# Block-window attention with FFN on one core: values ahead of scores, output projections one slot sooner, and the softmax maximum as a ScalarE bias in the last four slots

## What is computed

```python
xw   = blocks of 16 queries; keys/values: the first token plus 3 blocks (own and two before), masked
sim  = (x Wq * 64**-0.5) (x Wk)^T                    # 16 x 49 useful columns, masked above the diagonal
attn = softmax(sim)                                  # maximum subtracted
attn = einsum('gh,bhnij->bgnij', w_th, attn)         # heads mixed after the softmax
o    = (attn (x Wv)) Wo + b_out
x1   = layernorm(x + o)
h    = gelu(rms_norm(x1) ternary(w_up)^T)            # 128 -> 512
y    = layernorm(x1 + rms_norm(h) ternary(w_down)^T)
```

## Time and profile before

| | us |
|---|---|
| median of 3 runs (241.25 to 242.36) | 241.5 |
| the profiled execution, its own time | 243.09 |
| its span in the profile | 241.3 |
| busy in it: TensorE matmul / DVE / ScalarE / GpSimd | 226.1 / 176.6 / 164.1 / 92.6 |
| scores of slots 12, 16, 20, 24, 28 begin at | 82.06, 106.91, 132.92, 158.88, 185.08 |

### The profile page before, as it was taken

How to read it: one execution, slowest core, us unless ns; L and a number is a source line. 1 busy time by engine, 2 the same in 40 slices (tenths; PEclk the granted TensorE clock), 3 DMA queues, 4 the chain that set the end, 5 groups by cost and what they waited for, 6 DMA issues and landing times.

```text
span 241.3 us, 10011 instructions
## 1 busy us (share of the span) xinstructions
PE 226.1 (94%) x4343; PEld 203.1 (84%) x4343; DVE 176.6 (73%) x461; ACT 164.1 (68%) x311; POOL 92.6 (38%) x111
## 2 busy tenths in 40 slices
PE   7999899999999999999999999999999989989970
PEld 7899789888999999888988998888988977889750
DVE  0674699987777882688766885688468999785864
ACT  2686466776666648985599559964898334988652
POOL 7035204531343342444515454536254353120542
PEclk9999999999999999999999999999999999999975
DMA  6937560020020001100200111010201001000002
GB/s 217 293 101 209 165 139 7 7 61 3 3 58 13 24 3 39 35 21 8 65 3 4 48 34 36 3 46 4 68 3 29 20 3 46 1 4 22 3 3 87
DMA packets 19107, 11.69 MB, mean 48 GB/s; under 512 B 2232, under 2 KB 18168, under 8 KB 18936
## 3 DMA queue, kind: packets, MB, share of 16 engines
q1 hardware_dynamic: 18324, 10.47, 15.3%
q10 hardware_dynamic: 740, 0.59, 0.8%
HBM read 8.91 MB, written 2.10 MB: 46 GB/s over the span
## 4 chain that ended last, share of the span: by engine, by line
PE 57%; DVE 15%; ACT 8%; issue 7%; POOL 6%; SPq 2%; DMA 2%; POOLq 0%; DVEq 0%; ACTq 0%
PE bank L1108 9%; PE bank L1110 8%; PE bank L1109 8%; PE bank L1257 7%; PE bank L1231 6%; PE bank L1215 4%; DVE CTl L876 4%; POOL gTl L533 2%; DVE AT L881 2%; POOL xw L506 2%; DMA raw<-in_L_attn_x 2%; SPq L395 2%; DVE sm L896 2%; PE bank L1327 2%; PE bank L1189 2%
## 5 line engine op out<-in xcount | busy, mean ns | idle before, releaser
L577 ACT ACTIVATE Yb<-bank 128x512 f32<-128x512 f32 x64 | 38.4, 601 | 28.4 <-PE bank L1110 27.9
L519 POOL TENSOR_TENSOR E<-E,rc 128x400 f32<-128x400 f32 x32 | 27.9, 871 | 77.3 <-DVE rc L898 77.3
L876 DVE TENSOR_TENSOR CTl<-bank,CTh 128x512 fp32r<-128x512 f32 x64 | 41.1, 683 | 22.3 <-ACT CTh L577 22.1
L1108 PE MATMUL bank<-xTh,Gh 128*128 128x256 f32 x128 | 39.4, 308 | 1.7 <-ACT Yb L577 1.5
L1108 PE MATMUL bank<-CTh,Mh 128*128 128x256 f32 x128 | 37.0, 289 | 0.6 <-DVE CTl L876 0.6
L577 ACT ACTIVATE CTh<-bank 128x512 fp32r<-128x512 f32 x64 | 34.8, 600 | 2.5 <-PE bank L1257 2.4
L1110 PE MATMUL bank<-CTh,Ml 128*128 128x256 f32 x128 | 36.1, 282 | 0.0
L724 ACT ACTIVATE E<-E 128x400 f32<-128x400 f32 x32 | 17.3, 541 | 27.5 <-DVE E L890 27.4
L1109 PE MATMUL bank<-CTl,Mh 128*128 128x256 f32 x128 | 36.0, 281 | 0.0
L1109 PE MATMUL bank<-xTl,Gh 128*128 128x256 f32 x128 | 35.8, 280 | 0.0
L1110 PE MATMUL bank<-xTh,Gl 128*128 128x256 f32 x128 | 35.7, 279 | 0.0
(11 more groups left out here) (142 smaller groups left out, 469.3 us busy)
## 6 DMA issues: line engine op xcount, KB each, us to landing
raw<-in_L_attn_x SPq DMA_DIRECT2D x37, 64.0 KB
pt_rows<-PT SPq DMA_DIRECT2D x2, 512.0 KB, 4.7
R<-pt_rows SPq DMA_DIRECT2D x1, 1024.0 KB, 5.6
xr<-in_L_attn_x SPq DMA_DIRECT2D x6, 128.0 KB
out<-y SPq DMA_DIRECT2D x6, 128.0 KB, 1.9
raw<-in_L_attn_x SPq DMA_DIRECT2D x13, 56.0 KB
w_sb<-in_L_attn_w_qkv SPq DMA_DIRECT2D x2, 256.0 KB, 4.7
w_sb<-in_L_attn_w_qkv ACTq DMA_DIRECT2D x2, 256.0 KB, 4.5
```

Source lines behind the costliest of these rows:

```text
L519: tt(e, e, rc[s % 2][:, :].unsqueeze(2).broadcast_to([P, TILES, WIN]), ALU.mult).then_inc(s_norm, 1)
L577: copy = lambda o, i, **k: nc.scalar.activation(o, i, ACT.Copy, **k)
L876: v.tensor_tensor(ct_view(CTl[s // 4 % 2], s % 4, q), c_view(s, q), ct_view(f32(CTh[s // 4 % 2][:, :, :]), s % 4, q), ALU.subtract).then_i ...
L1108: mm(o, wh, rh, start=start, stop=False, **k)
```

## The change

Constants: `O_LAG` is 6, `TURN` 7, `BIASED` 28. From slot 8 on TensorE does `c_part(s-2)`, `scores(s)`, `transposes(s-1)`, the FFN's pieces, `queries(s, 0)`, `o_part` number `s-6`, `down`, `queries(s, 1)`. Slot 7 turns from the old order to the new one and does two projection parts; slot 31 also does two. `FIRST` is 10, 14, 18, 22, 26, 30, so each FFN step comes a slot sooner, chunk 4 stays in the loop until its square sum, and the special placements of chunks 3 and 4 are gone. `square_sum` stands inside `scores`, ahead of the mask matmul. GELU follows the exp directly. From slot 28 on DVE only changes the maximum's sign, and ScalarE computes exp straight from bank 0 in eight instructions, one per tile, with that as the bias; scores then wait for the exp of the slot before. The tail is rewritten, with 30 filler matmuls (`keep_busy`) where there were 5.

The tables:

```diff
-O_LAG = 7
+O_LAG = 6
+TURN = 7
+BIASED = 28
...
-            if s < 28:
-                return [divmod(s - O_LAG, 4)] if s >= O_LAG else []
-            return {28: [(5, 1), (5, 2)], 29: [(5, 3)], 30: [(6, 0)], 31: []}[s]
-        FIRST = [11 + 4 * n for n in range(5)] + [30]
+            if s < TURN:
+                return []
+            early = {7: [(0, 0), (0, 1)], 31: [(6, 1), (6, 2)]}
+            return early.get(s, [divmod(s - O_LAG, 4)])
+        FIRST = [10 + 4 * n for n in range(6)]
```

ScalarE's loop, slot s:

```diff
-                if s > LAG:
+                if LAG < s <= TURN:
                     ct_hi(s - LAG - 1)
...
+                if s >= TURN:
+                    ct_hi(s - 2)
+                    at_hi(s - 1)
...
                 act.wait_ge(s_sub, s + 1)
-                nc.scalar.activation(e, e, ACT.Exp).then_inc(s_exp, 1)
-                if s >= O_LAG:
+                if s < BIASED:
+                    nc.scalar.activation(e, e, ACT.Exp).then_inc(s_exp, 1)
+                else:
+                    for tile in range(TILES):
+                        ins = nc.scalar.activation(E[s % 2][:, tile, 0:WIN], bank[S_BANK][:, WIN * tile:WIN * tile + WIN],
+                                                   ACT.Exp, bias=mx[s % 2][:, tile:tile + 1])
+                    ins.then_inc(s_exp, 1)
+                for n, k in ffn(s):
+                    if k == 2:
+                        gelu(n, 0)
+                        gelu(n, 1)
+                if s >= TURN:
                     y_out(s, 1)
```

DVE, in `shift(s)` and then in its loop:

```diff
-                v.tensor_tensor(E[k][:, :, 0:WIN], scores, mx[k][:, :].unsqueeze(2).broadcast_to([P, TILES, WIN]),
-                                ALU.subtract).then_inc(s_sub, 1)
+                if s < BIASED:
+                    v.tensor_tensor(E[k][:, :, 0:WIN], scores, mx[k][:, :].unsqueeze(2).broadcast_to([P, TILES, WIN]),
+                                    ALU.subtract).then_inc(s_sub, 1)
+                else:
+                    v.tensor_scalar(mx[k][:, :], mx[k][:, :], -1.0, None, ALU.mult).then_inc(s_sub, 1)
...
+                if s > TURN:
+                    ct_lo(s - 2)
+                shift(s)
                 for n, k in ffn(s):
-                    if k == 5 and n == 3:
+                    if k == 5:
+                        dve.wait_ge(f_back, n + 1)
                         hidden_sum(n)
+                if s >= TURN:
+                    at_lo(s - 1)
```

TensorE, `scores` and its loop:

```diff
-            def scores(s):
+            def scores(s, sums=()):
                 need(pe, s_sub, s)
+                if s > BIASED:
+                    pe.wait_ge(s_exp, s)
...
+                for n in sums:
+                    pe.wait_ge(f_dS, n + 1)
+                    square_sum(n)
...
-                if s >= LAG:
+                if LAG <= s <= TURN:
                     transposes(s - LAG)
-                scores(s)
+                if s > TURN:
+                    c_part(s - 2)
+                scores(s, [n for n, k in ffn(s) if k == 5])
+                if s > TURN:
+                    transposes(s - 1)
...
-                if s >= LAG:
+                if LAG <= s < TURN:
                     c_part(s - LAG)
```

TensorE's tail behind `up` of chunk 6, old and new order:

```diff
-            attn_back(7)
-            down(4)
-            down(5)
-            down_back(4)
-            square_sum(4)
-            down(6)
-            down_back(5)
-            x1_T(7)
-            square_sum(5)
-            down_back(6)
-            up(7, 0)
-            up(7, 1)
-            square_sum(6)
-            keep_busy(2, 5)
+            down(5)
+            attn_back(7)
+            down_back(5)
+            square_sum(5)
+            keep_busy(1, 4)
+            down(6)
+            square_sum(6)
+            keep_busy(1, 4)
+            x1_T(7)
+            down_back(6)
+            keep_busy(1, 6)
+            up(7, 0)
+            up(7, 1)
+            keep_busy(1, 16)
             down(7)
             square_sum(7)
             down_back(7)
```

More of the change, by code:

```diff
@@ L310, in ss_bank @@
             return bank[O_BANK] if n >= 5 else dn_bank(n)
-        def c_bank(s, q):
-            return bank[(0, 2)[q] if s == 30 else C_BANK[q]]
         def y_bank(s, b):
@@ L318, in squared @@
         def squared(n):
-            return gT[0] if n < 4 else gT[2] if n % 2 else gsq
+            return gT[0] if n < 5 else gT[2] if n % 2 else gsq
         def gset(n):
@@ L345, in c_view @@
         def c_view(s, q):
-            return c_bank(s, q)[:, :].rearrange("p (r h s) -> p r h s", r=2, s=BLK)
+            return bank[C_BANK[q]][:, :].rearrange("p (r h s) -> p r h s", r=2, s=BLK)
         def f32(ap):
@@ L547, in _ @@
                 for n, k in ffn(s):
-                    if k == 4 and n < 4:
+                    if k == 4:
                         hidden_low(n, 0)
@@ L736, in _ @@
                         x1_hi(n)
-                    if k == 3 and n < 4:
+                    if k == 3:
                         hidden_high(n, 0)
                         hidden_high(n, 1)
-                    if k == 2 and n < 4:
-                        gelu(n, 0)
-                        gelu(n, 1)
-                    if k == 8 and n < 3:
+                    if k == 8:
                         result(n)
-            at_hi(30)
-            ct_hi(29)
-            gelu(4, 0)
+            x1_hi(5)
+            ct_hi(30)
             at_hi(31)
-            ct_hi(30)
-            gelu(4, 1)
+            stage(6)
             ct_hi(31)
-            x1_hi(5)
-            stage(6)
-            hidden_high(4, 0)
-            hidden_high(4, 1)
-            squares(4, 0)
-            squares(4, 1)
             gelu(5, 0)
@@ L762, in _ @@
             hidden_high(5, 1)
-            result(3)
             x1_hi(6)
+            result(4)
             squares(5, 0)
             stage(7)
+            squares(5, 1)
             gelu(6, 0)
@@ L770, in _ @@
             hidden_high(6, 1)
-            down_out(4)
-            squares(5, 1)
             down_out(5)
@@ L1018, in _ @@
                         up_input(n)
-                shift(s)
-                for n, k in ffn(s):
-                    if k == 5 and n < 3:
-                        hidden_sum(n)
-                    if k == 5 and n == 3:
-                        second_sum(n)
-                    if k == 6 and n == 3:
-                        second_norm(n)
-                    if k == 0 and n == 5:
-                        residual(n)
                 if s == STEPS - 1:
@@ L1256, in c_part @@
                             row = slice(64 * q, 64 * q + WIN)
-                            ins.append(mm(c_bank(s, q)[:, col], xw[s // 4 % 2][row, m, c, :], AT[row, a, col],
+                            ins.append(mm(bank[C_BANK[q]][:, col], xw[s // 4 % 2][row, m, c, :], AT[row, a, col],
                                           start=(n == 0), stop=(n == 2)))
@@ L1344, in _ @@
             for s in range(STEPS):
-                if 0 < s < O_LAG:
+                if 0 < s < TURN:
                     queries(s, 0)
@@ L1360, in _ @@
                         attn_back(n)
[L1361 removed]
+                    if k == 2:
                         up(n, 0)
                         up(n, 1)
[L1364 removed]
+                if s == 0 or s >= TURN:
                     queries(s, 0)
[L1366 to L1369 removed]
+                if s == TURN:
                     pe.wait_ge(s_eva, read_no("A", "m", 3))
@@ L1373, in _ @@
                     o_part(*part)
+                    if part == (0, 0):
+                        c_part(s - 2)
+                        transposes(s - 1)
                 for n, k in ffn(s):
-                    if k == 4 and n < 4:
+                    if k == 4:
                         down(n)
```

94 lines of the change are left out of this document (37 added, 57 removed).

## The result

The changed kernel takes **262.0 us** (median of 4 runs, 259.9 to 263.9), the kernel before beside it 241.9 (4 runs, 241.3 to 242.9): ratio 1.080, 95% interval 1.069 to 1.090. The forecast had the sign and the mechanism right and the size wrong: 254.4 was forecast, 12.9 over the median of 241.5 that it went by; 262.0 came, 20.0 over the 241.9 beside it and beyond the range's upper end of 259.5. Ratios are of fast runs alone, which leaves out one slow run of the changed kernel (without it the median is 260.6), three of e6 (241.0) and one of e9 (257.3).

What follows compares the result with a forecast made beforehand. TensorE, busy 94% of the span, was taken as the bound. Middle 5.9, slots 28 to 31 3.05 and 1.9, tail 0.1 and clock 2.0 sum to +12.9 over 241.5: 254.4 us, range 246.5 to 259.5.

Steps and rivals of the forecast that it cites:

- +2.66: At any slot's scores, values 0.91, a projection part 1.44 and FFN 0.31 more are done: work moved, no loss.
- +5.9: Middle slots: 9.3 us of added waits at `down` less 3.4 us of removed gaps.
- GpSimd's queue is where this collides: `hidden_low` stands directly behind the high half that awaits raw rows; `down` waits 4.1, 1.1, 1.1 and 3.0 us.
- Rivals 3 and 4: 3: GpSimd's collision hidden, only the end pays, 243, chance 0.08. 4: faster, TensorE alone bounds, 237.3, chance 0.07.
- rival 1: The stalls come but the clock stays at 2.4 GHz: 252.4 us, chance 0.28.
- rival 2: Clock falls in three places and loads cost more, or DVE and GpSimd slow each other: about 258 us, chance 0.12.
- one fall, a bit shorter: TensorE's clock is taken to fall once because of the stalls, costing +2.0 us; bounds 0 and 7.8.
- A fall costs at most 2.6 us: Upper cost of one clock fall, from 5.2 us of slower transposes at the kernel's start.
- at least as empty: Stalls of 4.1 and 3.0 us, and slots 29 and 30, compared with the tail microsecond where the clock falls.
- `down` at 16.65: Windows 5 and 6: TensorE reaches `down` 16.65 us into slot 16's or 20's count, so waits 1.1 each.
- 3.05 and 1.9: Slots 28 to 31: +3.05 us from added waits, +1.9 from chunk 4's FFN work ahead of the last projection.
- it starts 9.3 after the projection's end, not 7.0 (+2.3): Tail: last `up` starts 2.3 us later relative to the projection, the rest is 2.15 shorter; net +0.1.

Runs made afterwards that it cites:

- e6: e4 with chunk 4's GELU made a plain copy, so without its table loads: 241.5 us, ratio 0.9953.
- e9: The changed kernel with only the tail edits of e5: 258.6 us, ratio 1.0639.
- e3: The changed kernel with 26 filler matmuls ahead of `down` in slots 14 and 26: 256.6 us, ratio 1.0602.
- e1: The changed kernel with GpSimd's high half of windows 3 to 7 one slot later, behind `hidden_low`: 245.5 us, ratio 1.0145.
- e4: The changed kernel with the edits of e1 and e2 together (late high half, no bias part): 244.6 us, ratio 1.011.
- e5: e4 with the tail reordered on TensorE and ScalarE and ten fillers fewer: 239.4 us, ratio 0.9875.
- e2: The changed kernel with only the bias part undone (VectorE subtracts the maximum, one exp per slot): 259.3 us, ratio 1.0692.

## Why the prediction was right in kind and wrong in size

The profiled execution's 17.5 us, cut at three points that both traces have (scores of slots 12 and 28, end of the last chunk's projection, which is where the prediction cut as well):

| stretch | before | after | change | forecast |
|---|---|---|---|---|
| to scores of slot 12 | 82.06 | 84.02 | +2.0 | +2.66 |
| to scores of slot 28 | 103.0 | 115.25 | **+12.2** | +5.9 |
| to the projection's end | 35.1 | 36.5 | +1.4 | +2.3 |
| to the end of the span | 21.1 | 23.0 | **+1.9** | +0.1 |
| clock, wherever it falls | | (in the rows above) | | +2.0 |

**The collision was read rightly.** Waits of 4.1, 1.1, 1.1 and 3.0 were forecast, from start to start. Measured in the same way, e3 less e1, they are 4.0, 2.2, 1.4 and 3.1: 10.8 against 9.3 in all. The step "GpSimd's queue is where this collides" stands, by the trace and by e1: it needed only the order of one queue and the fact that the fetch waits for the low half. Rivals 3 and 4, in which that wait is hidden or never comes, fall, and so does rival 1, with a clock that stays up. The second half of rival 2, that VectorE and GpSimd slow each other, has no support: GpSimd's pieces take 2.39 to 2.41 and 2.49 to 2.51 us, before 2.40 and 2.55. Window 4 came 1 us sooner than I had it (high half at 100.44, not 101.4), since slot 12 itself stood 0.7 earlier.

**The failed step is the clock's +2.0: "one fall, a bit shorter".** It fell in slot 14 *and* in slot 26, in slot 30, and in the tail. By e3 the first two cost 2.1 and 2.5, the one in the tail 1.1 and the one in slot 30 nothing here: 5.7 in all, where 2.0 stood. "A fall costs at most 2.6 us" held, with some luck; the count did not. The 2.6 is half of some 5 us of slower transposes at the kernel's start, whose granted-clock rows read 1.00, and the two falls of the middle lasted 6.8 us each, so that they could have cost more. I had written that the two long stalls, and slots 29 and 30, were "at least as empty" as the place in which the clock falls in the kernel before, and then charged for one. By the rows there was no reason to count the second at nothing, as both were of one size in the end (2.90 and 2.57 in one piece). Rival 2 had the three places and a chance of 0.12; even its 258 was too low, because what the waits and the tail cost beyond the forecast was missing as well. The Trainium skill's rule ("TensorE: Matmul & The Clock Gate", Part 1), that idleness takes the clock away and sustained work gives it back, agrees with the trace here: the long waits did cost, each time.

**The middle without the clock was 7.2, not 5.9.** In e3, in which the clock is full, it takes 110.3. The waits are the whole of the 1.3: 10.8 less the 3.5 of gaps that e1 shows won is 7.3. Nearly all of the miss is in slots 18 and 22. The low halves came when forecast (16.9 and 18.2 us into slot 16 were forecast, TensorE's two steps start at 17.0 and 18.2), but "`down` at 16.65" is wrong: TensorE was there at 15.8 in slot 16's count and 15.7 in slot 20's, about 0.9 sooner, and waited so much longer. That the return transposes ahead of the hidden sum cost nothing is nearly borne out: e1 has the same order, and its middle is shorter than before by all of the gaps, with four small waits of 0.21 to 0.24 for the low weights in it.

**Slots 28 to 31: forecast +2.3 (3.05 and 1.9, less the 2.66 done sooner), measured +1.4; the pieces roughly right.** Values of slot 28 waited 1.68 (forecast 1.6), scores 0.41 (0.6), the projection 0.65 (0.55), and the transposes 0.42 to 0.50 (0.75 and 0.7); the wait of 0.75 for scores 31 did not come, but stands in e3 with 0.71. Eight exps took 1.65 (forecast 1.8). That GELU 4 between two exps is worse than the bias is not shown: the medians say so (3.1 in e6 against 0.9 in e4 beside e1), but the traces, up to the projection's end and with no fall in e4 and e6, have 1.2 for the GELU's tables and 2.5 for the bias. The page of the Trainium skill that spoke against this part harder, "ScalarE: Activation LUTs", What ACT_TABLE_LOAD costs, with a drain of 1.38 us behind each load, is again not borne out: the load at 203.68 ends at 204.96, and GELU starts at 204.97.

**The tail was costed at +0.1 and lost 1.9, and a better order recovers 3.8 of it.** The step that failed is "it starts 9.3 after the projection's end, not 7.0 (+2.3). From there on [...] 12.05 to the end, not 14.2 (-2.15)". It started 10.5 after it, and 12.5 were left. In e3, where the clock does not fall in the tail, the two are 9.8 and 12.1: the fall is 1.1 of the miss, and the work and waits ahead of the last `up` 0.5. I summed work there and did not look at ScalarE's queue, where `down_out(5)` stands behind chunk 6's halves and makes TensorE wait 1.59 (239.61). In the order of e5 and e9 the last `up` starts 7.0 after the projection's end.

**Between the profiled execution and the medians** lie 2.5 us more (20.0 against 17.5). The profiled execution of before lies 1.2 above the median beside the change (1.6 above the one that the forecast used); that of after lies 1.3 below its own. The changed kernel's runs spread over 4.0 us, those of before beside them over 1.7. Falls that come and go are the likely cause: the windows of e9 and the change at 160 show one that comes in one execution and not in another, and the time goes with each run's mean clock. The change's two slowest runs (263.3 and 263.9) have 0.943 and 0.950, its two fastest 0.954 and 0.978, and e4's ten part into two groups in the same way. Which falls the other executions had is not shown, as they have no trace. Waits at `down` are not needed for it: e1 and e4 have none and spread by 3.2 and 3.4 us; e5, whose tail has lost the wait of 1.59, spreads by 0.55.

Shares of the change by medians, each from its own experiment, so that they overlap and do not add up, with what the traces have in brackets: the order on GpSimd's queue with what it does to the clock 16.5 (15.8 in the middle), of the clock alone 5.4 (5.7); the tail 3.4 to 5.2 (3.8 to 4.1); GELU 4 between exps 3.1 (1.2); the bias 0.9 to 2.7 (1.5 to 2.5). They come to more than 20 because the order is sound once they are mended: e5 is 2.8 us faster than the kernel before.

## What to carry to other kernels

Moving a step one slot sooner moves it past everything on each queue that it uses: look for the instruction on that queue that waits for a transfer, and put nothing behind it that TensorE needs soon. Cost each idle stretch of TensorE of some 3 us twice, once as the wait and once as the clock behind it (2.1 and 2.5 us here), and count every such stretch. When two medians differ by less than their runs spread, compare the traces stretch by stretch, and look where the clock fell in each. When the middle has changed, read the tail's order again: what its last chain hangs on should be next in the queue when it is ready.

## What the runs showed of the chip that I had not expected

- A wait of 2.6 to 2.9 us in one piece, in the middle of dense work, brought the 1.2 GHz level for 6.8 us each, 2.1 and 2.5 us of time. In e2 waits of 2.9 and 3.1 brought it for 3.4 us each (from 104.2 and from 189.5). 26 matmuls of fillers (3.27 us) in the wait's place kept the clock at 1.00 and took nothing from the kernel.
- In e4 a wait of 1.99 in slot 30 left the clock alone, in e5 the same wait of 1.99 brought it down from about 193.8 to 197.2; in e1 and the change 1.67 and 1.68 brought it down, in e3 1.67 did not. So a wait of this size can go either way; no run here settles on what that hangs.
- What a fall costs depends on what else sets the pace. With the bias, a fall in slot 30 cost nothing (36.6 us up to the projection's end in e1 with it and in e3 without). Without the bias it cost 0.9: e4 and e5 are the same up to there and take 34.1 without and 35.0 with it.
- One exp of 400 columns taken as eight of 50, with a bias of one column each, took 1.65 us, some 0.19 apart.
